# Block rounding laid out by position in the block, with its powers of two held in 16 bits

## The chip, the cores and the metric

The kernel runs on 1 core of one Trainium2 chip. The metric is the device time of one execution in microseconds. The engines are named as in the profile: PE (matrix product; PEld is its weight load), DVE (vector), ACT (scalar), POOL, and SP, which issues DMAs.

## The reference

Two decoder layers run on x, 8 sequences of 256 rows of 512 numbers; each layer has attention, a second mixing and a feed-forward part, each behind a layer norm, each added to x. What is touched here is layer 0's feed-forward part. Its three products round both operands in blocks of 32 numbers along the summed axis: a power of two is taken from the block's largest magnitude, and each element is rounded to a tiny float format at that scale.

```
def _quantize_mx(x, ebits, mfrac, emax_elem, max_norm):
    xb = x.reshape(shp[:-1] + (shp[-1] // BLOCK, BLOCK))          # BLOCK = 32
    amax = jnp.max(jnp.abs(xb), axis=-1, keepdims=True)
    sexp = jnp.floor(jnp.log2(jnp.where(amax == 0, 1.0, amax))) - emax_elem
    scale = jnp.exp2(jnp.clip(sexp, -127.0, 127.0))
    return (_quantize_elem(xb / scale, ebits, mfrac, max_norm) * scale).reshape(shp)

_q_act = lambda x: _quantize_mx(x, 2, 3.0, 2.0, 7.5)
_q_w   = lambda w: _quantize_mx(w, 2, 1.0, 2.0, 6.0)
_mx_linear = lambda x, w: einsum('bsh,oh->bso', _q_act(x), _q_w(w))

gate, up = _mx_linear(x, w_gate), _mx_linear(x, w_up)     # 512 -> 2048
return _mx_linear(silu(gate) * up, w_down)                # 2048 -> 512
```

A permutation of the summed axis leaves the product as it is, so long as both operands have the same one.

## The kernel before

One program interleaves all parts. For each engine a string of letters (`TURNS0`) says which stream of work issues its next step; `side_by_side` follows it. A stream is a generator, and a step is what stands between two `yield`s. So the order of each engine's instructions is fixed when the kernel is built, and semaphores hold an engine where its operand isn't there yet. On DVE, letter g steps the weights' rounding (`Quantised.dve`), f the feed-forward part (`Hidden.dve`), b, d and e the attention, the mixing and the norm beside them. Layer 0 reaches to about 1000 us, layer 1 from about 920 us to the end.

**Weights, once.** `Quantised` takes 12 units of [128, 2048] f32: four of `gate`, four of `up`, four of `down`. SP loads a unit into one of two raw buffers. DVE then works in steps: the maximum of each block (L794), its bounds and the exponent e and inverse (L797 to L801, three small instructions in one step), times the inverse (L805), the element's own exponent (L808, L811), an added and subtracted constant that rounds (L814, L817), and last the lower bound and the block's power of two into `w16`, bf16 (L822). PE transposes `w16` in 16 pieces of 128 columns (L834), ACT copies them out of PSUM (L851). Before it writes `w16`, L822 waits for `w_ps`, PE's transposes of the unit before.

**Activations, 8 sequences.** For each sequence `Hidden.dve` rounds five times 1024 numbers per partition: once the normed rows (two row tiles of 512), and four times half a tile of the product of silu and up. That is 40 roundings. One has two steps. `dve_quantise`: maximum of 32 blocks (L1133), its bounds (L1135), e (L1137), inverse (L1139), and the source times the inverse into `z8`, whose fp8 type does the rounding (L1142). `dve_rounded`: bounds from fp8 to bf16 (L1148), then times e (L1150), which lets PE begin the transposes (L1164, L1192) and then the products (L1178, L1204). e and the inverse are f32, one number for each block, and are read with step 0 along the 32 elements:

```
own(nc.vector.tensor_scalar(dst, self.z8[:, :], 7.5 / 64, -7.5 / 64, ALU.min, ALU.max))
own.wait()
nc.vector.tensor_tensor(blocks(dst), blocks(dst), broadcast(self.e[:, :], 2, BLOCK), ALU.mult
                        ).then_inc(self.s["q_ready"], 1)
```

`own` counts DVE's own instructions, and `own.wait()` holds the next one until they are through. POOL multiplies silu and up (L1296) and hides what attention may not see (L737).

Of the kernel before, what the change touches and what calls it, by code (L numbers as in the profile page):

```python
# [6 lines left out]
BF16 = mybir.dt.bfloat16  # L7
F16 = mybir.dt.float16
FP8 = mybir.dt.float8e4
I32 = mybir.dt.int32  # L10
ALU = mybir.AluOpType
# [138 lines left out]
def build(nc, x, ctx_rows, ctx_cols, A, F, M, G, Xd, out):  # L150
# [17 lines left out]
    with top:  # L168
        def sb(stack, name, shape, dt=F32):
            return stack.enter_context(nc.sbuf_tensor(name, shape, dt))  # L170
# [589 lines left out]
        class Quantised:  # L760


            def __init__(self, st, banks, room, gate16, up16, down16):
                self.b = banks
                self.gate16, self.up16, self.down16 = gate16, up16, down16
                self.raw = [room[:, 2048 * i:2048 * i + 2048] for i in range(2)]
                self.c = room[:, 4096:6144]
                self.w16 = room[:, 6144:7168].bitcast(BF16)
                self.q_max, self.q_e, self.q_inv, _ = (
                    sb(st, f"w_{part}", [P, 2048 // BLOCK])[:, :] for part in ("max", "e", "inv", "sc"))  # L770
                self.raw_in = [sem(f"w_raw_in{i}") for i in range(2)]
# [16 lines left out]
            def dve(self, dve, own, i):  # L788
# [10 lines left out]
                own(nc.vector.tensor_scalar(q_e.bitcast(I32), q_max.bitcast(I32), EXPONENT, None, ALU.bitwise_and))  # L799
                own.wait()  # L800
                mark = own(nc.vector.tensor_scalar(q_inv.bitcast(I32), q_e.bitcast(I32), -1.0, float(256 << 23),  # L801
# [307 lines left out]
        class Hidden:  # L1109


            def __init__(self, st, banks, mixing, room, quantised, gate16, up16, down16):
# [3 lines left out]
                                    for a in range(2))  # L1116
# [7 lines left out]
                self.m, self.e, self.inv, _ = (sb(st, f"ffn_{part}", [P, 1024 // BLOCK])  # L1124
                                                     for part in ("m", "e", "inv", "sc"))
# [4 lines left out]
            def dve_quantise(self, dve, own, src):  # L1130
                m, e, inv = (t_[:, :] for t_ in (self.m, self.e, self.inv))
                blocks = lambda t_: t_.rearrange("p (n b) -> p n b", b=BLOCK)
                own(nc.vector.tensor_reduce(m, blocks(src), AX.X, ALU.max, apply_absolute_value=True))  # L1133
# [3 lines left out]
                own(nc.vector.tensor_scalar(e.bitcast(I32), m.bitcast(I32), EXPONENT, None, ALU.bitwise_and))  # L1137
                own.wait()
                own(nc.vector.tensor_scalar(inv.bitcast(I32), e.bitcast(I32), -1.0, float(250 << 23),  # L1139
                                            ALU.mult, ALU.add))  # L1140
                own.wait()
# [3 lines left out]
            def dve_rounded(self, dve, own, at, dst):  # L1145
                blocks = lambda t_: t_.rearrange("p (n b) -> p n b", b=BLOCK)
# [99 lines left out]
            def dve(self, dve, own, n):  # L1246
# [5 lines left out]
                self.dve_quantise(dve, own, self.xn[:, :, :].rearrange("p t d -> p (t d)"))  # L1252
                yield
                self.dve_rounded(dve, own, 5 * n, self.iq[0][:, 0:1024])
                for g in range(TT * FB + 2):
# [17 lines left out]
                    self.dve_quantise(dve, own, self.inter[q % 2])  # L1273
                    yield
                    self.dve_rounded(dve, own, 5 * n + q + 1, self.iq[T][:, 1024 * half:1024 * half + 1024])
# [764 lines left out]
```

## Time and profile before

| | |
|---|---|
| median of 3 runs | 1605.75 us (1604.0 to 1606.85) |
| the profiled execution | 1603.94 us |
| its span, first to last instruction | 1602.2 us |
| busy in the span | PE 85%, DVE 83%, ACT 65%, POOL 27% |
| the chain that ended last | PE 47%, DVE 29%, ACT 10%, issue 7%, POOL 4% |
| DVE from 15.8 to 1000 us | 866.8 us busy of 984.2 |

The profile is of one execution. Busy time says how full an engine is; the chain of waits, followed back from the last instruction, says which work the end waited for. Both are read by stretch, since the change lies between 15 and 976 us alone.

### The profile page before, as it was taken

The numbers are of one execution on the slowest core, as the hardware profiler recorded it, in microseconds if no ns is written. First come the engines' busy times: TensorE is split into PE (matmuls) and PEld (weight loads), VectorE is DVE, ScalarE is ACT, GpSimd is POOL, SyncE is SP. The second block draws the span as 40 slices with busy tenths as digits, with TensorE's granted clock in tenths as the row PEclk, the third lists the DMA queues.
The fourth block names the chain that finished last, engine by engine and source line by source line (L and its number), as shares of the span: only waits on it lengthen the run. The fifth ranks groups of instructions, "written<-read, shape, count | busy, mean of one in ns | idle before, by whom it ended". The sixth has DMA issues, their size and how long they took to land.

```text
span 1602.2 us, 32850 instructions
## 1 busy us (share of the span) xinstructions
PE 1361.3 (85%) x13068; PEld 745.7 (47%) x13068; DVE 1332.5 (83%) x1965; ACT 1037.2 (65%) x1884; POOL 428.2 (27%) x495
## 2 busy tenths in 40 slices
PE   3778878879899999898978767879999998999986
PEld 2454535344445453444443333446555555555643
DVE  6988989979879888887798899888788888978743
ACT  3244365465673865765695769886899788989431
POOL 1432141132240422321331240241222313122310
PEclk9697989799999999999999988889999999999988
DMA  6313122200201111002120003011020211101020
GB/s 223 93 54 93 34 68 68 74 15 1 75 15 41 36 41 42 21 22 54 63 89 28 1 1 132 20 41 44 2 71 13 59 39 33 41 5 44 2 81 27
DMA packets 54201, 76.24 MB, mean 48 GB/s; under 512 B 8480, under 2 KB 23840, under 8 KB 53536
## 3 DMA queue, kind: packets, MB, share of 16 engines
q1 hardware_dynamic: 54048, 74.14, 16.2%
q8 instruction: 104, 1.70, 0.4%
q14 instruction: 49, 0.40, 0.1%
HBM read 38.98 MB, written 9.44 MB: 30 GB/s over the span
## 4 chain that ended last, share of the span: by engine, by line
PE 47%; DVE 29%; ACT 10%; issue 7%; POOL 4%; DMA 1%; SPq 1%; ACTq 0%; DVEq 0%; POOLq 0%
PE bank L200 16%; DVE mix_NM L1079 4%; PE bank L1178 4%; PE bank L534 3%; DVE ssm_HS L1537 2%; PE bank L542 2%; PE bank L522 2%; PE bank L992 2%; PE bank L1204 2%; PE bank L557 2%; DVE ffn_m L1133 2%; PE bank L977 2%; POOL attn_P L737 2%; PE bank L495 1%; DVE ffn_Z L1142 1%
## 5 line engine op out<-in xcount | busy, mean ns | idle before, releaser
L1052 ACT ACTIVATE mix_P<-bank 128x512 f32<-128x512 f32 x256 | 142.3, 604 | 50.6 <-PE bank L977 50.2
L1079 DVE TENSOR_REDUCE mix_NM<-bank 128x2 f32<-128x512 f32 x256 | 162.8, 682 | 11.2 <-PE bank L952 10.4
L737 POOL TENSOR_SCALAR_AFFINE_SELECT cross_P<-cross_P 128x256 f32<-128x256 f32 x128 | 90.5, 717 | 272.9 <-ACT cross_P L642 272.4
L1296 POOL TENSOR_TENSOR ffn_room<-ffn_room 128x512 f32<-128x512 f32 x64 | 89.9, 1406 | 263.9 <-ACT ffn_room L1235 167.0
L1537 DVE TENSOR_TENSOR_SCAN ssm_HS<-ssm_DA,ssm_DD 128x1024 f32<-128x1024 f32 x64 | 150.3, 2348 | 10.1 <-ACT ssm_DD L1488 5.5
L737 POOL TENSOR_SCALAR_AFFINE_SELECT attn_P<-attn_P 128x256 f32<-128x256 f32 x128 | 89.6, 713 | 243.7 <-ACT attn_P L642 243.7
L1485 ACT ACTIVATE ssm_DA<-ssm_Z,A_T 128x255 f32<-128x255 f32 x256 | 110.9, 498 | 3.1 <-DVE ssm_HS L1537 2.7
L642 ACT ACTIVATE attn_P<-bank 128x384 f32<-128x384 f32 x128 | 63.8, 498 | 63.1 <-PE bank L523 62.7
L642 ACT ACTIVATE cross_P<-bank 128x384 f32<-128x384 f32 x128 | 62.6, 489 | 50.9 <-PE bank L523 50.5
L1543 DVE TENSOR_TENSOR ssm_HS<-ssm_HS,ssm_CS 128x1024 f32<-128x1024 f32 x64 | 82.0, 1281 | 0.9
L1460 ACT ACTIVATE ssm_Z<-bank 128x512 f32<-128x512 f32 x128 | 72.2, 599 | 13.4 <-PE bank L1374 12.8
L1178 PE MATMUL bank<-gate,ffn_XQ 128*128 128x512 bf16 x256 | 68.8, 392 | 13.0 <-DVE ffn_room L1260 12.7
L992 PE MATMUL bank<-mix_P,mix_V 128*32 128x256 f32 x1024 | 69.6, 395 | 2.8 <-DVE mix_XN L1095 2.2
L1178 PE MATMUL bank<-up,ffn_XQ 128*128 128x512 bf16 x256 | 68.5, 392 | 0.5 <-ACT ffn_room L1235 0.5
L977 PE MATMUL bank<-mix_Q,mix_K 64*128 64x256 f16 x512 | 53.2, 288 | 18.3 <-ACT mix_P L1052 15.6
L1488 ACT ACTIVATE ssm_DD<-ssm_Z 128x1024 f32<-128x1024 f32 x64 | 67.2, 1050 | 0.0
L952 PE MATMUL bank<-mix_K,mix_Q 64*128 64x256 f16 x512 | 51.6, 281 | 16.6 <-DVE mix_NM L1079 15.1
L1204 PE MATMUL bank<-down,ffn_room 128*128 128x512 bf16 x256 | 64.9, 389 | 0.0
L1231 ACT ACTIVATE ffn_room<-bank 128x512 f32<-128x512 f32 x64 | 38.9, 607 | 34.3 <-PE bank L1178 34.1
L1260 DVE SCALAR_TENSOR_TENSOR ffn_room<-ffn_room,bank 128x512 f32<-128x512 f32 x64 | 43.5, 680 | 19.3 <-ACT ffn_room L1231 19.3
L522 PE MATMUL bank<-attn_stack 128*128 128x256 f16 x128 | 39.1, 305 | 21.9 <-ACT attn_P L642 16.6
L1150 DVE TENSOR_TENSOR ffn_room<-ffn_room,ffn_e 128x1024 bf16<-128x1024 bf16 x40 | 54.3, 1357 | 1.4
(410 smaller groups left out, 4043.3 us busy)
## 6 DMA issues: line engine op xcount, KB each, us to landing
attn_stack<-attn_P SPq DMA_DIRECT2D x96, 128.0 KB, 2.4
cross_stack<-cross_P SPq DMA_DIRECT2D x96, 128.0 KB, 2.4
ffn_room<-f_gate SPq DMA_DIRECT2D x4, 1024.0 KB, 5.3
XR<-x SPq DMA_DIRECT2D x8, 512.0 KB, 6.8
ffn_room<-f_up SPq DMA_DIRECT2D x4, 1024.0 KB, 5.6
ffn_room<-f_down SPq DMA_DIRECT2D x4, 1024.0 KB, 4.9
x_mid<-XR SPq DMA_DIRECT2D x8, 512.0 KB, 3.0
XR<-x_mid SPq DMA_DIRECT2D x8, 512.0 KB, 3.7
```

The source lines that it names most:

```text
L200: last = nc.tensor.matmul(out, a_, b_, start=(start and i == 0), stop=(stop and i == len(terms) - 1))
L642: nc.scalar.activation(self.p[h % 8][:, :], bank[self.b[0]][:, 0:S + P], ACT.Exp, scale=HD1 ** -0.5).then_inc(self.p_ready, 1)
L737: nc.gpsimd.affine_select(out=diagonal, in_=diagonal, compare_op=ALU.is_ge, fill=0.0, base=0, pattern=[[0, 2], [1, P]], channel_multiplier ...
L977: last = nc.tensor.matmul(bank[b4[i]][:, k * S:(k + 1) * S], self.k[rows, v // 2, k * P:(k + 1) * P], self.q[rows, v, :], start=(k == 0), ...
L992: last = nc.tensor.matmul(bank[b][32 * j:32 * j + 32, half * S:(half + 1) * S], self.v[:, k, g, :], self.p[(4 * g + j) % 8][:, k * S:(k + ...
L1052: nc.scalar.activation(self.p[h % 8], bank[b4[h % 2]][:, :], ACT.Exp, scale=HD2 ** -0.5).then_inc(s["p_ready"], 1)
L1079: nc.vector.tensor_reduce(self.nm[:, t, 16 * i + 2 * g:16 * i + 2 * g + 2], bank[b4[u % 3]][:, :].rearrange("p (c k) -> p c k", c=2), AX.X ...
L1178: last = nc.tensor.matmul(bank[b][:, :], self.xq[:, k, T * P:(T + 1) * P], w[:, k, fb * 512:(fb + 1) * 512], start=(k == 0), stop=(k == DC ...
L1204: last = nc.tensor.matmul(bank[b][:, :], self.iqt[:, f, :], self.down16[:, f, :], start=(f == 0), stop=(f == FC - 1))
L1296: nc.gpsimd.tensor_tensor(self.inter[q % 2][:, 512 * (g % 2):512 * (g % 2) + 512], self.sg[g % 2], self.up[g % 2], ALU.mult).then_inc(s["i ...
L1485: nc.scalar.activation(self.da[:, G % 2, k, 1:S], self.z[:, h, 1:S], ACT.Exp, scale=self.A_T[:, h:h + 1])
L1537: nc.vector.tensor_tensor_scan(flat(self.hs), flat(self.da), flat(self.dd), 0.0, ALU.mult, ALU.add).then_inc(s["hs_ready"], 1)
```

## The change

The elements of a group of blocks are stored by their position in the block: first element 0 of every block of the group, then element 1, and so on. A group is 16 blocks (512 numbers) for the normed rows, `gate` and `up`, and 32 blocks (1024 numbers) for the product of silu and up, and `down`. With this the factor of each block runs along the innermost axis with step 1, and the 32 positions repeat the row.

- e and the inverse are bf16. Their bits are made as 16-bit integers from the upper half of each f32 maximum.
- Activations: the product with the inverse reads the f32 source 32 numbers apart and writes `z8` in order. The bounds are as before. The last product has dst, source and e in bf16, all of step 1. For the normed rows (8 of the 40) the bounds on the maximum are left out (`bounded=True`).
- Weights: the added constant has no upper bound of 6 in it any more (`tensor_tensor` in place of `scalar_tensor_tensor`); the subtraction reads both f32 operands 32 numbers apart and writes bf16 straight into `w16`; a new `tensor_scalar` bounds `w16` on both sides; the last product is bf16 by bf16. The wait for `w_ps` stands before the subtraction, since that is now the first to write `w16`.
- PE, ACT, POOL, SP and `TURNS0` are the same.

```diff
@@ Quantised.__init__
-                self.q_max, self.q_e, self.q_inv, _ = (
-                    sb(st, f"w_{part}", [P, 2048 // BLOCK])[:, :] for part in ("max", "e", "inv", "sc"))
+                self.q_max = sb(st, "w_max", [P, 2048 // BLOCK])[:, :]
+                self.q_e, self.q_inv = (sb(st, f"w_{part}", [P, 2048 // BLOCK], BF16)[:, :] for part in ("e", "inv"))
@@ Quantised.dve
-                own(nc.vector.tensor_scalar(q_e.bitcast(I32), q_max.bitcast(I32), EXPONENT, None, ALU.bitwise_and))
+                own(nc.vector.tensor_scalar(q_e.bitcast(I16), q_max.bitcast(I16)[:, 1::2], EXPONENT >> 16, None,
+                                            ALU.bitwise_and))
...
-                mark = own(nc.vector.scalar_tensor_tensor(y, y, 6.0, c, ALU.min, ALU.add))
-                yield
-                own.wait(mark)
-                mark = own(nc.vector.tensor_tensor(y, y, c, ALU.subtract))
-                yield
+                mark = own(nc.vector.tensor_tensor(y, y, c, ALU.add))
+                yield
+                n = (1024 if self.units[i][1] == "down" else D) // BLOCK
+                positions = self.w16.rearrange("p (a b n) -> p a b n", b=BLOCK, n=n)
+                y_, c_ = (t_.rearrange("p (a n b) -> p a b n", n=n, b=BLOCK) for t_ in (y, c))
                 own.wait(mark)
                 if i:
                     dve.wait_ge(self.w_ps, 2 * i)
-                nc.vector.scalar_tensor_tensor(blocks(self.w16), blocks(y), -6.0, broadcast(q_e, 2, BLOCK), ALU.max,
-                                               ALU.mult).then_inc(self.w16_ready, 1)
+                mark = own(nc.vector.tensor_tensor(positions, y_, c_, ALU.subtract))
+                yield
+                own.wait(mark)
+                own(nc.vector.tensor_scalar(self.w16, self.w16, 6.0, -6.0, ALU.min, ALU.max))
+                own.wait()
+                nc.vector.tensor_tensor(positions, positions, broadcast(q_e.rearrange("p (a n) -> p a n", n=n), 2, BLOCK),
+                                        ALU.mult).then_inc(self.w16_ready, 1)
@@ Hidden.dve_quantise
-                own(nc.vector.tensor_scalar(m, m, TINY, HUGE, ALU.max, ALU.min))
+                if not bounded:
+                    own(nc.vector.tensor_scalar(m, m, TINY, HUGE, ALU.max, ALU.min))
+                    own.wait()
+                own(nc.vector.tensor_scalar(e.bitcast(I16), m.bitcast(I16)[:, 1::2], EXPONENT >> 16, None,
+                                            ALU.bitwise_and))
...
-                nc.vector.tensor_tensor(blocks(self.z8[:, :]), blocks(src), broadcast(inv, 2, BLOCK), ALU.mult,
-                                        saturate=False).then_inc(self.s["z_ready"], 1)
+                nc.vector.tensor_tensor(self.by_position(self.z8[:, :], n), src.rearrange(
+                    "p (a n b) -> p a b n", n=n, b=BLOCK), self.each_position(inv, n), ALU.mult, saturate=False
+                    ).then_inc(self.s["z_ready"], 1)
@@ Hidden.dve_rounded
-                nc.vector.tensor_tensor(blocks(dst), blocks(dst), broadcast(self.e[:, :], 2, BLOCK), ALU.mult
-                                        ).then_inc(self.s["q_ready"], 1)
+                nc.vector.tensor_tensor(self.by_position(dst, n), self.by_position(dst, n),
+                                        self.each_position(self.e[:, :], n), ALU.mult).then_inc(self.s["q_ready"], 1)
```

DVE's instructions at weight unit 1, the second unit, with the semaphores that hold them: before,

```order
L814 SCALAR_TENSOR_TENSOR ffn_room<-ffn_room 128x2048 [waits done_dve]
L679 TENSOR_REDUCE attn_NM<-bank 128x4 [waits attn_rest_ready,attn_s_ps] x4
L683 TENSOR_REDUCE attn_NM<-bank 128x2 [waits attn_s_ps] x8
L817 TENSOR_TENSOR ffn_room<-ffn_room 128x2048 [waits done_dve]
L688 SCALAR_TENSOR_TENSOR attn_NQL<-bank,attn_NQH 32x256 [waits attn_nqh_ready]
L822 SCALAR_TENSOR_TENSOR ffn_room<-ffn_room,w_e 128x2048 [waits w_ps,done_dve]
```

and with the change, where all line numbers are those of the changed kernel:

```order
L816 TENSOR_TENSOR ffn_room<-ffn_room 128x2048 [waits done_dve]
L680 TENSOR_REDUCE attn_NM<-bank 128x4 [waits attn_rest_ready,attn_s_ps] x4
L684 TENSOR_REDUCE attn_NM<-bank 128x2 [waits attn_s_ps] x8
L824 TENSOR_TENSOR ffn_room<-ffn_room 128x2048 [waits w_ps,done_dve]
L689 SCALAR_TENSOR_TENSOR attn_NQL<-bank,attn_NQH 32x256 [waits attn_nqh_ready]
L827 TENSOR_SCALAR ffn_room<-ffn_room 128x2048 [waits done_dve]
L829 TENSOR_TENSOR ffn_room<-ffn_room,w_e 128x2048 [waits done_dve]
```

The wait for `w_ps` has moved from the last instruction of the unit to the subtraction, ahead of the small attention instruction (L688 before, L689 after). The last step has two instructions in place of one.

## Rows read from the trace of the kernel before

**Rows 1.** The page, its sections 1 and 4 (busy times; the chain of waits).
```profile
PE 1361.3 (85%) x13068; PEld 745.7 (47%) x13068; DVE 1332.5 (83%) x1965; ACT 1037.2 (65%) x1884; POOL 428.2 (27%) x495
...
PE 47%; DVE 29%; ACT 10%; issue 7%; POOL 4%; DMA 1%; SPq 1%; ACTq 0%; DVEq 0%; POOLq 0%
```

**Rows 2.** Busy time in three stretches: us, then each engine's busy time (xinstructions).
```profile
core 0: us, PE busy (x) PEld busy (x) DVE busy (x) ACT busy (x) POOL busy (x), PEclk, DMA share, GB/s
15.80:53.00 37.20, 24.39 (x147) 16.08 (x147) 36.75 (x27) 15.27 (x26) 16.35 (x11) 0.91 0.40 127
53.00:370.00 317.00, 251.78 (x2634) 141.77 (x2635) 282.80 (x346) 158.56 (x294) 82.54 (x87) 0.85 0.21 60
370.00:1000.00 630.00, 548.23 (x4984) 271.27 (x4982) 547.27 (x844) 419.07 (x756) 179.14 (x193) 0.97 0.14 41
```

**Rows 3.** The chain of waits by line, from 370 to 1000 us.
```profile
by line: PE bank L1178 10.1%; issue 8.8%; DVE mix_NM L1079 7.9%; PE bank L200 7.6%; PE bank L1204 4.2%; DVE ffn_m L1133 3.8%; PE bank L992 3.6%; DVE ffn_Z L1142 3.5%; DVE ffn_room L1150 3.4%; PE bank L952 2.8%; DVE ffn_room L1148 2.7%; ACT 
```

**Rows 4.** The chain of waits by line, from 15.8 to 53, then from 53 to 370 us.
```profile
by line: DVE ffn_room L805 12.1%; DVE ffn_room L811 12.1%; DVE w_max L794 11.8%; DVE ffn_room L808 9.8%; DVE ffn_room L822 6.2%; DVE ffn_room L814 6.0%; DVE ffn_room L817 5.9%; DVE l_wo_l L292 5.9%; DVE l_wq_l L292 5.9%; DVE l_wk_l L292 5.9
...
by line: PE bank L200 9.4%; issue 8.8%; POOL attn_P L737 7.6%; DVE mix_NM L1079 5.3%; ACT attn_P L642 4.4%; PE bank L522 4.3%; PE bank L534 4.2%; PE bank L542 3.5%; PE bank L992 3.5%; PE bank L495 3.2%; PE bank L977 2.7%; PE bank L834 2.4%;
```

**Rows 5.** Groups of DVE instructions: xcount | busy us, mean ns of one | idle before.
```profile
L1150 DVE TENSOR_TENSOR ffn_room<-ffn_room,ffn_e 128x1024 bf16<-128x1024 bf16 x40 | 54.3, 1357 | 1.4
...
L1133 DVE TENSOR_REDUCE ffn_m<-ffn_room 128x32 f32<-128x1024 f32 x40 | 48.4, 1210 | 2.0 <-ACT ffn_room L357 1.6
...
L1135 DVE TENSOR_SCALAR ffn_m<-ffn_m 128x32 f32<-128x32 f32 x40 | 13.7, 343 | 1.4
```

**Rows 6.** Single lines of the activations' rounding: ns min/median/max, first and last start, forms.
```profile
L1142 DVE TENSOR_TENSOR ffn_Z<-ffn_room,ffn_inv x40: 1224/1225/2274, 367.7 to 974.1; 128x1024 fp8e4<-128x1024 f32 x40
...
L1150 DVE TENSOR_TENSOR ffn_room<-ffn_room,ffn_e x40: 1224/1226/3252, 371.4 to 976.1; 128x1024 bf16<-128x1024 bf16 x40
...
L1148 DVE TENSOR_SCALAR ffn_room<-ffn_Z x40: 628/693/2309, 370.7 to 975.3; 128x1024 bf16<-128x1024 fp8e4 x40
...
L1135 DVE TENSOR_SCALAR ffn_m<-ffn_m x40: 181/182/1307, 367.1 to 973.4; 128x32 f32<-128x32 f32 x40
```

**Rows 7.** The same for lines of the weights' rounding.
```profile
L817 DVE TENSOR_TENSOR ffn_room<-ffn_room x12: 2269/2282/2519, 35.7 to 352.7; 128x2048 f32<-128x2048 f32 x12
...
L822 DVE SCALAR_TENSOR_TENSOR ffn_room<-ffn_room,w_e x12: 2270/2293/4485, 38.0 to 358.3; 128x2048 bf16<-128x2048 f32 x12
...
L811 DVE TENSOR_SCALAR ffn_room<-ffn_room x12: 1162/1220/3252, 27.8 to 343.7; 128x2048 f32<-128x2048 f32 x12
```

**Rows 8.** The same for the scan of the second layer, another kind of work.
```profile
L1537 DVE TENSOR_TENSOR_SCAN ssm_HS<-ssm_DA,ssm_DD x64: 2269/2284/3375, 922.8 to 1484.3; 128x1024 f32<-128x1024 f32 x64
```

**Rows 9.** Timeline round weight unit 1: start us, us, engine, line [idle before <-releaser].
```profile
57.47 5.01 DVE L683 TENSOR_REDUCE attn_NM<-bank 128x2 f32<-128x512 f32 x8
...
61.68 1.03 PE L834 MATMUL bank<-ident,ffn_room 128*128 128x128 bf16 x8
62.39 2.28 DVE L817 TENSOR_TENSOR ffn_room<-ffn_room 128x2048 f32<-128x2048 f32 x1
...
62.94 1.06 PE L834 MATMUL bank<-ident,ffn_room 128*128 128x128 bf16 x8
...
64.59 0.41 DVE L688 SCALAR_TENSOR_TENSOR attn_NQL<-bank,attn_NQH 32x256 f16<-32x256 f32 x1
...
67.72 0.37 PE L522 MATMUL bank<-attn_stack 128*128 128x256 f16 x1 [3.72 <-issue]
```

**Rows 10.** DVE alone in time, one rounding of activations and what stands in it.
```profile
482.95 1.21 DVE L1133 TENSOR_REDUCE ffn_m<-ffn_room 128x32 f32<-128x1024 f32 x1
...
484.84 1.23 DVE L1142 TENSOR_TENSOR ffn_Z<-ffn_room,ffn_inv 128x1024 fp8e4<-128x1024 f32 x1
...
486.58 0.68 DVE L1148 TENSOR_SCALAR ffn_room<-ffn_Z 128x1024 bf16<-128x1024 fp8e4 x1
487.30 1.23 DVE L1150 TENSOR_TENSOR ffn_room<-ffn_room,ffn_e 128x1024 bf16<-128x1024 bf16 x1
```

More of the change, by code:

```diff
@@ L10 @@
 I32 = mybir.dt.int32
+I16 = mybir.dt.int16
 ALU = mybir.AluOpType
@@ L1123, in __init__ @@
                 self.z8 = sb(st, "ffn_Z8", [P, 1024], FP8)
-                self.m, self.e, self.inv, _ = (sb(st, f"ffn_{part}", [P, 1024 // BLOCK])
-                                                     for part in ("m", "e", "inv", "sc"))
+                self.m = sb(st, "ffn_m", [P, 1024 // BLOCK])
+                self.e, self.inv = (sb(st, f"ffn_{part}", [P, 1024 // BLOCK], BF16) for part in ("e", "inv"))
                 names = ("th_ready", "z_ready", "q_ready", "xqt_ps", "xqt_ready", "gu_ps", "silu_ready", "up_ready", "in_done",
@@ L1128, in __init__, with dve_quantise @@
                 self.s = {part: sem(f"ffn_{part}") for part in names}
[L1130 to L1133, printed above, removed]
-                own.wait()
-                own(nc.vector.tensor_scalar(m, m, TINY, HUGE, ALU.max, ALU.min))
+            def dve_quantise(self, dve, own, src, groups, bounded=False):
+                m, e, inv = self.m[:, :], self.e[:, :], self.inv[:, :]
+                n = 1024 // BLOCK // groups
+                own(nc.vector.tensor_reduce(m, src.rearrange("p (n b) -> p n b", b=BLOCK), AX.X, ALU.max,
+                                            apply_absolute_value=True))
+                own.wait()
+                if not bounded:
[3 more added lines that the diff above has]
+                                            ALU.bitwise_and))
@@ L1136, in dve_quantise @@
                 own.wait()
-                own(nc.vector.tensor_scalar(e.bitcast(I32), m.bitcast(I32), EXPONENT, None, ALU.bitwise_and))
+                own(nc.vector.tensor_scalar(inv.bitcast(I16), e.bitcast(I16), -1.0, float(250 << 7), ALU.mult, ALU.add))
                 own.wait()
-                own(nc.vector.tensor_scalar(inv.bitcast(I32), e.bitcast(I32), -1.0, float(250 << 23),
-                                            ALU.mult, ALU.add))
-                own.wait()
-                nc.vector.tensor_tensor(blocks(self.z8[:, :]), blocks(src), broadcast(inv, 2, BLOCK), ALU.mult,
-                                        saturate=False).then_inc(self.s["z_ready"], 1)
@@ L1145, in dve_rounded, with by_position @@
-            def dve_rounded(self, dve, own, at, dst):
-                blocks = lambda t_: t_.rearrange("p (n b) -> p n b", b=BLOCK)
+                nc.vector.tensor_tensor(self.by_position(self.z8[:, :], n), src.rearrange(
+                    "p (a n b) -> p a b n", n=n, b=BLOCK), self.each_position(inv, n), ALU.mult, saturate=False
+                    ).then_inc(self.s["z_ready"], 1)
+            def by_position(self, rows, n):
+                return rows.rearrange("p (a b n) -> p a b n", b=BLOCK, n=n)
@@ L1147, in dve_rounded, with each_position @@
+            def each_position(self, scale, n):
+                return broadcast(scale.rearrange("p (a n) -> p a n", n=n), 2, BLOCK)
+            def dve_rounded(self, dve, own, at, dst, groups):
+                n = 1024 // BLOCK // groups
                 dve.wait_ge(self.s["z_ready"], at + 1)
@@ L1251, in dve @@
                     dve.wait_ge(s["iqt_ps"], 4 * n - 2)
-                self.dve_quantise(dve, own, self.xn[:, :, :].rearrange("p t d -> p (t d)"))
+                self.dve_quantise(dve, own, self.xn[:, :, :].rearrange("p t d -> p (t d)"), TT, bounded=True)
                 yield
-                self.dve_rounded(dve, own, 5 * n, self.iq[0][:, 0:1024])
+                self.dve_rounded(dve, own, 5 * n, self.iq[0][:, 0:1024], TT)
                 for g in range(TT * FB + 2):
@@ L1272, in dve @@
                     dve.wait_ge(s["q_ready"], 5 * n + q + 1)
-                    self.dve_quantise(dve, own, self.inter[q % 2])
+                    self.dve_quantise(dve, own, self.inter[q % 2], 1)
                     yield
-                    self.dve_rounded(dve, own, 5 * n + q + 1, self.iq[T][:, 1024 * half:1024 * half + 1024])
+                    self.dve_rounded(dve, own, 5 * n + q + 1, self.iq[T][:, 1024 * half:1024 * half + 1024], 1)
                     if q == 3:
```

2 lines of the change are left out of this document (1 added, 1 removed).

## The prediction

> **What bounds the kernel now.** First the page: PE and DVE are both busy for over 80% of the span, and the chain that ended last runs 47% over PE and 29% over DVE [rows 1]. No one engine bounds it. All that the change touches lies between 15 and 976 us, so the page's shares are no use and I read stretches. From 15.8 to 53 us DVE is busy 36.75 of 37.2 us, from there to 370 us 282.8 of 317, from 370 to 1000 us 547.27 of 630 [rows 2]: 99%, 89%, 87%. DVE has little room in layer 0, and PE has as little from 370 us on (548.23).
>
> Next, how much of the touched work the end waited for. From 370 to 1000 us the chain spends 3.8% of 630 us, 23.9 us, in L1133 [rows 3], whose 40 instructions take 48.4 us [rows 5]: half of the roundings of activations are on the chain. L1142 (3.5%) and L1150 (3.4%) say the same. For the weights the first 37 us are almost all DVE in the chain, with L817 and L822 at about 6% each, one of either; from 53 to 370 us neither is among the lines listed, the last of which has 2.4% [rows 4], 7.6 us. L817 and L822 have 11 instructions each there, about 25 us, so under three tenths of each.
>
> Last, the durations. An f32 instruction of 1024 numbers takes 1.225 us, one of 2048 2.282 us, so a further number costs 1.03 ns, which I call one beat, and an instruction some 0.17 us besides [rows 6, 7]. L1150 is bf16 into bf16 but has an f32 factor: 1.226 us, one number per beat. L1148, one source, moves 1024 in 0.693 us: two per beat. The scan takes 2.284 us for 1024: two beats per number [rows 8].
>
> **The activations' last product, L1150.** With all three operands 16 bits wide and in runs of 16 or 32, I take two numbers per beat, L1148's 0.69 us. A gain of 0.53 us, 40 times: 21.3 us less on DVE. The other end is 1.226 us and no gain. Its mean is 1.357, not 1.226 [rows 5], so some instances are held up, and that I leave as it is.
>
> **The bounds left out** for 8 of 40: 0.18 us each by the median [rows 6], 1.5 us; by the mean of 0.343 [rows 5], 2.7 us. The integer steps on e and the inverse are as many as before and of the same small size: nothing.
>
> **The product into z8, L1142.** Same operation, same count, but its f32 source is now read 32 numbers, 128 bytes, apart, at each element. No DVE row in this trace does that in SBUF on a large instruction: all go along rows in runs of 16 or more. Lower end: the hop is free and it stays 1.225 us. Upper end: the rate of the scan, two beats, 2.284 us, and for a worse case three beats, about 3.3 us. I take the scan's 2.28 us, that is 1.06 us more. The choice isn't forced by a row; what speaks for it is that wherever more than one number per beat is reached (L1148, L811) neighbours in memory are read, so a read fetches more than one number, and a hop per element wastes that. 40 times 1.06 is 42.4 us more on DVE.
>
> The Trainium skill speaks to this and against the change: "DVE Microarchitecture Reference", section "Measured stream behaviour on trn2", says that a port keeps its full rate only where successive elements come in runs of at least two adjacent 4-byte words, and gives 1.05 ns per column for such runs, 1.73 for one source hopping at each element, and 2.50 where both sources step by 24 words. An estimate by that page: L1142 would cost 0.7 to 1.5 us more in place of 1.06, the weights' subtraction 1.4 to 3.0 us more, and by the same sum as below the kernel would land between 1616 and 1640 us. No row of this trace shows it.
>
> For the activations then: +42.4 - 21.3 - 1.5 = +19.6 us on DVE. Half of the roundings are on the chain: **+9.8 us**. At 482.95 us a rounding stands in a stretch where DVE has no gap between its instructions [rows 10]: what grows there pushes all behind it, so half is the low side for a lengthening. Before a sequence's rounding is late, L1178's and L1204's products on PE are next to be late.
>
> **The weights.** Per unit: L814 loses its bound and keeps its time. L817 reads two hopping sources: by the same choice two beats for 2048, 4.4 us, +2.1 (ends 0 and three beats, +4.2). L822 from 2.293 to 1.22, since two per beat for 2048 is L1142's time for 1024 now: -1.07 (other end 0). The new instruction on bf16 lies between L811's 1.22 us and L1148's 0.69, which would be four per beat; I take 0.70, since one source at 16 bits should have both gains. Sum +1.75 us, 12 times: +21 us on DVE. Unit 0 is on the chain: +1.75. Unit 1's subtraction stands ahead of L688, and that ahead of SP's DMA and of L522, before which PE stands idle for 3.72 us [rows 9]: +2.1 on the chain. The other ten: three tenths of 17.5, +5.3. Together **+9.1 us**.
>
> **The moved wait.** In every unit but unit 1 (and unit 4, by a little) PE's transposes of the unit before were over long before the subtraction. At unit 1 the subtraction starts at 62.39 us and PE's last eight transposes of unit 0 end at 62.94 + 1.06 = 64.00 [rows 9]. The subtraction now waits: +1.6 us, and behind it on DVE wait L688 and so L522. **+1.6 us**. After a slower unit 0 the same wait simply moves along.
>
> **Sum.** 9.8 + 9.1 + 1.6 = 20.5 us on the profiled execution's 1603.94: 1624.4. The median is 1.8 us higher: 1626 us, 1.3% slower. About 0.2% (3 us) is what a measurement of this kernel can tell from no change.
>
> **Rivals.**
> - *The hop is free.* DVE loses 21.3 + 1.5 on the activations, half of it on the chain, -11.4 us; on the weights -0.37 per unit, unit 0 and three tenths of the rest, -1.6 us; the moved wait stays, +1.6. -11.4 us: about 1594, faster. For it: no row shows a slow hop, and the change is only in addresses. It decides if L1142's successor is at 1.23 us; the point of no gain is at about 1.6 us, where the growth of the two hopping instructions eats the rest. Chance 0.18.
> - *The hop costs about half a beat*, and gain and loss cancel on the activations, while the weights bring a few us: 1606 to 1609. Chance 0.07 to be within 0.2%.
> - *The last product isn't faster*, because its factor is a repeated row of 16 or 32: it stays one per beat, with slow hops. 21.3 us come back on DVE, half on the chain, and 1.07 for each weight unit: +10.6 and +4.6. 1641 us. L1148, with two per beat, speaks against it but has no such factor. Chance 0.1.
> - *Three beats*, or DVE's growth of 40 us drags nearly all roundings onto the chain, since it was at 87 to 89%: with all of +19.6 and +21 counted, 1646; with three beats and seven tenths on the chain, 1672. Chance 0.15.
> - The forecast itself, two beats give or take a third: 0.5.
>
> **Range and chances.** The forecast's own case, L1142 at 0.7 to 1.4 us more and the subtraction at twice that, gives by the same sum +10 to +31 us: 1616 to 1637. The range takes in the free hop at its lower end, and at the upper the growth that is on the chain as a whole: 1594 to 1650. Left out are three beats and a free hop with luck. Faster 0.18, same 0.07, slower 0.75.
>
> **What would show it.** In the changed kernel's profile: the z8 product at 2.28 us (free: 1.23), the last product at 0.69 (no gain: 1.23), the weights' subtraction at 4.4 us, its last product at 1.22, the new instruction at 0.70. DVE's busy time up by about 40 us; from 370 to 1000 us its share above 87%, and more of L1133's line in the chain than 3.8%. At weight unit 1 DVE idle for about 1.6 us before the subtraction, released by PE's transposes. The prediction is wrong if the z8 product stays below 1.6 us, or if DVE grows as told and the span doesn't: then the roundings had more slack than the chain's half says.

## The result: 1.6% slower, and the profile after

The changed kernel took 1634.43 us (median of 4 runs, 1633.79 to 1635.03) against 1605.83 us (1604.0 to 1606.85) in the same comparison: ratio 1.0158, interval 1.0136 to 1.018. The forecast was 1626 us, slower; 1634.4 lies in the range of 1594 to 1650. Its profiled execution took 1633.79 us with a span of 1632.1. One of the four executions of the changed kernel with a second buffer (e9, below) took 1954.07 us at a mean granted clock of 0.641, where the others had 0.93, and its ratio leaves it out.

From the page of the changed kernel, busy times and the chain, to set against [rows 1]:

```profile
PE 1370.2 (84%) x13005; PEld 753.6 (46%) x13068; DVE 1353.4 (83%) x1969; ACT 1037.5 (64%) x1884; POOL 440.6 (27%) x495
...
PE 46%; DVE 31%; ACT 9%; issue 8%; POOL 4%; DMA 1%; SPq 0%; ACTq 0%; DVEq 0%; POOLq 0%
```

DVE is busy for 20.9 us more, PE for 8.9 although its work is the same and 63 of its records are missing here (its mean granted clock was 0.939 before and is 0.925 here). DVE's share of the chain has gone from 29 to 31%, which says little: the stretches and the single lines say more. First the touched lines, in the view of one line each (ns min/median/max, first and last start, forms), to set against [rows 6, 7]:

```profile
L1151 DVE TENSOR_TENSOR ffn_Z<-ffn_room,ffn_inv x40: 1880/1930/2910, 389.1 to 999.6; 128x1024 fp8e4<-128x1024 f32 x40
...
L1164 DVE TENSOR_SCALAR ffn_room<-ffn_Z x40: 629/693/2260, 392.7 to 1001.6; 128x1024 bf16<-128x1024 fp8e4 x40
...
L1166 DVE TENSOR_TENSOR ffn_room<-ffn_room,ffn_e x40: 691/693/2717, 393.4 to 1002.3; 128x1024 bf16<-128x1024 bf16 x40
...
L824 DVE TENSOR_TENSOR ffn_room<-ffn_room x12: 3953/4062/4204, 35.8 to 372.5; 128x2048 bf16<-128x2048 f32 x12
...
L827 DVE TENSOR_SCALAR ffn_room<-ffn_room x12: 657/744/3882, 39.9 to 378.9; 128x2048 bf16<-128x2048 bf16 x12
...
L829 DVE TENSOR_TENSOR ffn_room<-ffn_room,w_e x12: 1224/1226/1381, 43.8 to 379.6; 128x2048 bf16<-128x2048 bf16 x12
```

- L1151 is L1142's successor, with the source read 32 numbers apart: 1.930 us for 1.225.
- L1164 is L1148 and unchanged. L1166 is L1150's successor, all bf16 in step 1: 0.693 us for 1.226.
- L824 is L817's successor, two sources apart: 4.062 us for 2.282. L829, the weights' last product: 1.226 for 2.293.
- L827 is the new instruction on bf16: 0.744 us, but once 3.882; its mean, from the view of groups, is 1.17:

```profile
L827 DVE TENSOR_SCALAR ffn_room<-ffn_room 128x2048 bf16<-128x2048 bf16 x12 | 14.1, 1172 | 0.3
```

By medians one rounding of activations grew by 0.705 - 0.533 = 0.17 us, and one weight unit by 1.78 + 0.74 - 1.07 = 1.45 us. So the change gains on every last product what it was built to gain, and pays more than that where the operands are brought into the new order.

Where the time went is read by marks. The first maximum of activations starts at 365.8 us before and at 387.4 after; the last instruction of the last rounding starts at 976.1 [rows 6] and at 1002.3. Busy times in the two stretches, first before, then after (columns as in [rows 2]):

```profile
0.00:365.80 365.80, 272.86 (x2751) 155.30 (x2752) 317.55 (x370) 175.97 (x319) 101.87 (x123) 0.86 0.26 79
365.80:976.10 610.30, 534.40 (x4903) 266.00 (x4902) 528.30 (x833) 398.91 (x730) 179.14 (x193) 0.97 0.12 35
```

```profile
0.00:387.40 387.40, 279.38 (x2751) 159.01 (x2752) 335.68 (x382) 176.26 (x319) 110.57 (x123) 0.84 0.25 75
387.40:1002.30 614.90, 530.53 (x4841) 266.72 (x4902) 530.67 (x825) 398.95 (x731) 184.31 (x193) 0.97 0.12 34
```

Of 29.9 us of span, 21.6 are lost before the first rounding, in the time of the weights, with 18.1 us more DVE work; 4.6 in the roundings' stretch, with 2.4 us more; and 3.7 behind the last one, where the code is the same. Those last I don't take for an effect of the change. The last addition of layer 1, DVE writing `XR` (first and last start), before, after, and in a kernel with the code of before but for two types (below):

```profile
L1726 DVE TENSOR_TENSOR XR<-XR,bank x16: 660/683/690, 1133.5 to 1597.1; 128x512 f32<-128x512 f32 x16
```

```profile
L1742 DVE TENSOR_TENSOR XR<-XR,bank x16: 660/684/689, 1164.1 to 1626.9; 128x512 f32<-128x512 f32 x16
```

```profile
L1727 DVE TENSOR_TENSOR XR<-XR,bank x16: 660/684/689, 1138.1 to 1601.3; 128x512 f32<-128x512 f32 x16
```

From the last rounding to it: 621.0 us before, 624.6 after, 624.7 (1601.3 - 976.6) in the third, whose ratio to before is 1.0011. All eleven other profiles of this case lie between 623.3 and 625.9 us, so the one profile of before happened to have a short layer 1.

The stretches of [rows 2] in the changed kernel, and the chain of waits by line from 53 to 370 and from 370 to 1010 us, to set against [rows 3, 4]:

```profile
core 0: us, PE busy (x) PEld busy (x) DVE busy (x) ACT busy (x) POOL busy (x), PEclk, DMA share, GB/s
15.80:53.00 37.20, 24.97 (x147) 16.45 (x147) 36.82 (x25) 15.32 (x26) 15.96 (x11) 0.95 0.42 132
53.00:370.00 317.00, 242.33 (x2503) 133.84 (x2504) 281.85 (x336) 144.16 (x274) 88.74 (x86) 0.82 0.20 58
370.00:1000.00 630.00, 540.31 (x4930) 274.36 (x4991) 543.54 (x841) 409.75 (x743) 187.19 (x195) 0.96 0.12 34
```

```profile
by line: POOL attn_P L738 9.7%; PE bank L201 8.6%; issue 8.0%; DVE mix_NM L1086 6.8%; DVE ffn_room L824 4.4%; PE bank L535 4.1%; PE bank L496 3.9%; PE bank L543 3.3%; PE bank L485 2.8%; ACT attn_P L643 2.8%; PE bank L558 2.7%; PE bank L999 
...
by line: issue 11.1%; PE bank L1194 9.7%; DVE mix_NM L1086 8.6%; PE bank L201 7.3%; DVE ffn_Z L1151 5.9%; DVE ffn_m L1140 4.5%; PE bank L1220 3.1%; PE bank L959 2.7%; DVE ffn_room L1164 2.7%; ACT mix_P L1059 2.6%; PE bank L999 2.4%; DVE ffn
```

Cut at fixed times the stretches hide the change: DVE is as busy per stretch as before, since the work has moved later. In the chain one sees it: L824 with 4.4% of 317 us is 14 us, where L817 was under 2.4%; L1151 has 5.9% where L1142 had 3.5%, and L1140, the maximum, 4.5% where L1133 had 3.8% (the stretch here ends 10 us later).

DVE's timeline at weight units 0 and 1, to set against [rows 9]:

```profile
35.77 4.06 DVE L824 TENSOR_TENSOR ffn_room<-ffn_room 128x2048 bf16<-128x2048 f32 x1
39.87 3.88 DVE L827 TENSOR_SCALAR ffn_room<-ffn_room 128x2048 bf16<-128x2048 bf16 x1
...
60.98 5.01 DVE L684 TENSOR_REDUCE attn_NM<-bank 128x2 f32<-128x512 f32 x8
67.62 3.97 DVE L824 TENSOR_TENSOR ffn_room<-ffn_room 128x2048 bf16<-128x2048 f32 x1 [1.62 <-PE bank L841]
71.52 0.40 DVE L689 SCALAR_TENSOR_TENSOR attn_NQL<-bank,attn_NQH 32x256 f16<-32x256 f32 x1
```

At unit 1 DVE stands idle for 1.62 us before the subtraction, released by PE's transposes (L841): the moved wait as it was foretold. At unit 0 the new bf16 instruction takes 3.88 us in place of 0.7. In the changed kernel a POOL memset runs beside it:

```profile
39.69 3.51 POOL L408 MEMSET attn_stack<- 32x4096 f16 x1
```

In the old kernel the same memset (L407, from 39.58 us) ran beside L822 and L794, which took their usual 2.29 and 2.28 us. There two instructions of unit 1 were held up instead:

```profile
47.02 2.38 DVE L808 TENSOR_SCALAR ffn_room<-ffn_room 128x2048 int32<-128x2048 int32 x1
49.44 3.25 DVE L811 TENSOR_SCALAR ffn_room<-ffn_room 128x2048 f32<-128x2048 f32 x1
```

Their successors take 1.23 us each here, so about 3.2 us come back; but the small L798 and L803 take 1.63 and 2.22 us for 0.64 and 0.48, which costs 2.7 (L800 between them gives 0.8 back). At the next attention instruction, which started at 54.94 us before and starts at 58.45 here, DVE is 3.5 us later, 2 us more than the 1.45 of the medians. So such hold-ups fall on whichever instruction stands there. That POOL's work beside them is the cause is not shown; no run takes it away.

### The profile page after: what moved, and what is told of

It reads as the page before. It is cut to its first block, busy times and chain, and to the rows that moved or that the text cites. A ratio compares the mean times of both kernels' runs of the same rounds, so it can differ in the third digit from the quotient of the medians.

```text
span 1632.1 us, 32791 instructions
## 1 busy us (share of the span) xinstructions
PE 1370.2 (84%) x13005; PEld 753.6 (46%) x13068; DVE 1353.4 (83%) x1969; ACT 1037.5 (64%) x1884; POOL 440.6 (27%) x495
## 4 chain that ended last, share of the span: by engine, by line
PE 46%; DVE 31%; ACT 9%; issue 8%; POOL 4%; DMA 1%; SPq 0%; ACTq 0%; DVEq 0%; POOLq 0%
PE bank L201 16%; DVE mix_NM L1086 5%; PE bank L1194 4%; PE bank L535 3%; DVE ffn_Z L1151 2%; PE bank L543 2%; DVE ssm_HS L1553 2%; PE bank L496 2%; POOL attn_P L738 2%; PE bank L558 2%; PE bank L523 2%; DVE ffn_m L1140 2%; PE bank L1418 1%; PE bank L999 1%; PE bank L485 1%
## 5 line engine op out<-in xcount | busy, mean ns | idle before, releaser
L1312 POOL TENSOR_TENSOR ffn_room<-ffn_room 128x512 f32<-128x512 f32 x64 | 94.6, 1480 | 263.4 <-ACT ffn_room L1251 181.1
L738 POOL TENSOR_SCALAR_AFFINE_SELECT attn_P<-attn_P 128x256 f32<-128x256 f32 x128 | 96.0, 764 | 250.4 <-ACT attn_P L643 250.3
L1151 DVE TENSOR_TENSOR ffn_Z<-ffn_room,ffn_inv 128x1024 fp8e4<-128x1024 f32 x40 | 78.4, 1959 | 1.4
L1194 PE MATMUL bank<-gate,ffn_XQ 128*128 128x512 bf16 x227 | 63.6, 397 | 15.8 <-DVE ffn_room L1276 11.9
L1220 PE MATMUL bank<-down,ffn_room 128*128 128x512 bf16 x237 | 61.3, 389 | 1.5 <-issue 0.7
```

What stands on the lines that cost most here:

```text
L738: nc.gpsimd.affine_select(out=diagonal, in_=diagonal, compare_op=ALU.is_ge, fill=0.0, base=0, pattern=[[0, 2], [1, P]], channel_multiplier ...
L1151: nc.vector.tensor_tensor(self.by_position(self.z8[:, :], n), src.rearrange("p (a n b) -> p a b n", n=n, b=BLOCK), self.each_position(inv, ...
L1194: last = nc.tensor.matmul(bank[b][:, :], self.xq[:, k, T * P:(T + 1) * P], w[:, k, fb * 512:(fb + 1) * 512], start=(k == 0), stop=(k == DC ...
L1312: nc.gpsimd.tensor_tensor(self.inter[q % 2][:, 512 * (g % 2):512 * (g % 2) + 512], self.sg[g % 2], self.up[g % 2], ALU.mult).then_inc(s["i ...
```

## Experiments

I use the mark again: the start of the last rounding's last instruction, 976.1 us before. It leaves layer 1 out, which differs from run to run, but it is read from one profile of each kernel. The start of the first rounding is the other mark: 365.8 us before. "Over before" is worked out from the ratio.

**Theory A.** DVE is full before 390 us, and each microsecond it grows there is a microsecond of the kernel; the weights make most of the loss. **Theory B.** The activations' roundings, half on the chain, cost as much as the weights. **Theory C.** The moved wait ties DVE to PE's order and costs far more than its 1.6 us.

### The activations' part alone (e1_acts)

```diff
 the changed kernel, with class Quantised (the weights' rounding) as in the kernel before
```

> The activations' part of the change alone; the weights are rounded as before, in natural order, so the summed axes of the two operands no longer correspond. Theory A (DVE's growth before 390 us is what costs, and the weights make it): z8 product 1.93 us, last product 0.69, DVE busy +6 us, time 1606 to 1613 us. Theory B (the activations' roundings are half on the chain and hopping hurts there as much as in the weights): 1618 us or more.

Measured: 1613.27 us, ratio 1.0025 (1.0007 to 1.0044), 4 us over before. The z8 product and the last product:

```profile
L1145 DVE TENSOR_TENSOR ffn_Z<-ffn_room,ffn_inv x40: 1878/1934/2924, 368.2 to 981.4; 128x1024 fp8e4<-128x1024 f32 x40
...
L1160 DVE TENSOR_TENSOR ffn_room<-ffn_room,ffn_e x40: 691/693/2719, 372.5 to 984.1; 128x1024 bf16<-128x1024 bf16 x40
```

The durations are those of the whole change; the mark is 984.1 us, 8.0 later. DVE's busy time is 4.8 us up, 1337.3 for the 1332.5 of [rows 1]. That is A's size and not B's, which asked for 12 us or more.

### The weights' part alone (e2_weights)

```diff
 the kernel before, with class Quantised as in the changed kernel
```

> The weights' part alone; activations as before, in natural order, so the summed axes no longer correspond. Theory A: the first rounding of activations starts about 21 us later than before, time 1622 to 1632 us. Theory B: 1612 to 1618 us.

Measured: 1631.44 us, ratio 1.0137 (1.0115 to 1.0158), 22 us over before.

```profile
L824 DVE TENSOR_TENSOR ffn_room<-ffn_room x12: 3930/4050/4190, 35.7 to 373.2; 128x2048 bf16<-128x2048 f32 x12
...
L1157 DVE TENSOR_TENSOR ffn_room<-ffn_room,ffn_e x40: 1224/1226/3252, 393.8 to 999.0; 128x1024 bf16<-128x1024 bf16 x40
```

The mark is 999.0, 22.9 later. The weights' part makes the loss; B falls.

### The types without the order (e3_types)

```diff
-                self.m, self.e, self.inv, _ = (sb(st, f"ffn_{part}", [P, 1024 // BLOCK])
-                                                     for part in ("m", "e", "inv", "sc"))
+                self.m = sb(st, "ffn_m", [P, 1024 // BLOCK])
+                self.e, self.inv = (sb(st, f"ffn_{part}", [P, 1024 // BLOCK], BF16) for part in ("e", "inv"))
```

and e and the inverse made from 16-bit integers, as in the change.

> Before, with e and the inverse of the activations in bf16 but in natural order, the factor at step 0 along the 32 elements. If type alone gives two numbers per beat: last product 0.69 us, DVE busy -21 us, 1590 to 1600 us. If step 1 is needed (my theory): last product stays 1.226 us, z8 product 1.225 us, time within 3 us of before.

Measured: 1608.4 us, ratio 1.0011 (0.9994 to 1.0028), no difference.

```profile
L1143 DVE TENSOR_TENSOR ffn_Z<-ffn_room,ffn_inv x40: 1224/1225/2289, 368.4 to 974.6; 128x1024 fp8e4<-128x1024 f32 x40
...
L1151 DVE TENSOR_TENSOR ffn_room<-ffn_room,ffn_e x40: 1224/1226/3248, 372.0 to 976.6; 128x1024 bf16<-128x1024 bf16 x40
```

With the factor in bf16 but repeated at step 0 the last product stays at 1.226 us. The 0.693 needs the factor to run at step 1 (the change and the next run have it so), and the new order provides that.

### The same in pairs (e4_pairs, and once more)

The order is: pair of positions, block, element of the pair. Each f32 read then takes two neighbours before it hops, and e holds each value twice so that it still runs at step 1. Each instruction keeps three free dimensions, so the normed rows take two z8 products of 512, and a weight unit two or four subtractions. The weights have the same order, with PE and ACT as in the change.

```diff
-                own(nc.vector.tensor_scalar(e.bitcast(I16), m.bitcast(I16)[:, 1::2], EXPONENT >> 16, None,
-                                            ALU.bitwise_and))
+                own(nc.vector.tensor_scalar(e.bitcast(I16).rearrange("p (n t) -> p n t", t=2),
+                                            broadcast(m.bitcast(I16)[:, 1::2], 2, 2), EXPONENT >> 16, None,
+                                            ALU.bitwise_and))
...
-                nc.vector.tensor_tensor(self.by_position(self.z8[:, :], n), src.rearrange(
-                    "p (a n b) -> p a b n", n=n, b=BLOCK), self.each_position(inv, n), ALU.mult, saturate=False
-                    ).then_inc(self.s["z_ready"], 1)
+                for a in range(groups):
+                    part = slice(a * 1024 // groups, (a + 1) * 1024 // groups)
+                    last = nc.vector.tensor_tensor(
+                        self.z8[:, part].rearrange("p (b n t) -> p b n t", n=n, t=2),
+                        src[:, part].rearrange("p (n b t) -> p b n t", n=n, t=2),
+                        broadcast(inv[:, 2 * n * a:2 * n * (a + 1)].rearrange("p (n t) -> p n t", t=2), 1, BLOCK // 2),
+                        ALU.mult, saturate=False)
```

> The change with pairs of neighbouring elements kept together: the order is pair of positions, block, element of the pair, and e has each value twice. If the hop at each element is what slows the reads: z8 product 1.23 us for 1024 numbers, two of 0.69 for the normed rows, subtraction in pieces of 0.69 (512) or 1.23 us (1024), last products 0.69 and 1.23 us; DVE busy about 20 us below before and the time 1590 to 1603 us. If any order out of line costs: z8 product stays at 1.9 us and the time at 1630 us or above.

> The kernel with pairs once more, beside the next one: 0.988 to 0.993 of before.

Measured: 1593.54 us, ratio 0.9903 (0.988 to 0.9925); the second time 1596.4 us, 0.9932 (0.9906 to 0.9959). **Faster than before by 0.7 to 1.0%.** The new bf16 instruction, the weights' last product, the z8 product, and the activations' last product:

```profile
L831 DVE TENSOR_SCALAR ffn_room<-ffn_room x12: 672/694/1878, 38.4 to 359.1; 128x2048 bf16<-128x2048 bf16 x12
...
L834 DVE TENSOR_TENSOR ffn_room<-ffn_room,w_e x12: 1224/1226/1303, 40.3 to 359.8; 128x2048 bf16<-128x2048 bf16 x12
...
L1159 DVE TENSOR_TENSOR ffn_Z<-ffn_room,ffn_inv x48: 680/1224/2268, 368.3 to 961.3; 128x1024 fp8e4<-128x1024 f32 x32, 128x512 fp8e4<-128x512 f32 x16
...
L1176 DVE TENSOR_TENSOR ffn_room<-ffn_room,ffn_e x40: 691/693/2716, 372.0 to 963.3; 128x1024 bf16<-128x1024 bf16 x40
```

The z8 product is back at 1.224 us and the last products keep their gain. So it is the hop at every element that costs, not the order as such. Before the first rounding and from there to the last:

```profile
0.00:366.60 366.60, 271.86 (x2752) 154.88 (x2753) 318.22 (x411) 175.62 (x319) 96.55 (x123) 0.86 0.26 79
366.60:963.30 596.70, 529.34 (x4910) 264.78 (x4908) 507.00 (x833) 398.19 (x730) 176.61 (x193) 0.99 0.12 35
```

Up to the first rounding nothing is gained (318.2 us of DVE work for 317.6, since the subtraction in pieces and the new instruction use up what the last product gives). The roundings' stretch has 21.3 us less DVE work than before and is 13.6 us shorter: about two thirds of what DVE is relieved of passes into the time. PE's granted clock is 0.99 there for 0.97 before, so a part of the 13.6 may be PE's.

### The moved wait alone (e5_wait)

```diff
                 own.wait(mark)
+                if i:
+                    dve.wait_ge(self.w_ps, 2 * i)
                 mark = own(nc.vector.tensor_tensor(y, y, c, ALU.subtract))
                 yield
                 own.wait(mark)
-                if i:
-                    dve.wait_ge(self.w_ps, 2 * i)
```

> Before, with the wait for w_ps moved ahead of the weights' subtraction and nothing else. If the wait costs what the timeline shows: DVE idle 1.6 us at unit 1, first rounding of activations 1.5 to 4 us later, time 1 to 4 us over before. If the moved wait is what made most of the 21 us (rival: it ties DVE to PE's order): 10 us or more over before.

Measured: 1611.04 us, ratio 1.0016 (0.9997 to 1.0034). DVE's wait (us in total, times, longest), and the last product:

```profile
DVE ffn_room L819 <- PE bank L834: 2.0, 2, 1.6
...
L1150 DVE TENSOR_TENSOR ffn_room<-ffn_room,ffn_e x40: 1224/1226/3249, 377.2 to 980.9; 128x1024 bf16<-128x1024 bf16 x40
```

The stall is the foretold one. The mark is 980.9, 4.8 later, by one profile; the ratio gives 2.6 us, and its interval reaches from nothing to 5.5. C, with 10 us and more, falls.

The 4.8 us are more than DVE's 2.0 us of waiting, and the timelines show where the rest comes in. A unit's maximum (L794) starts at 83.88 us before and at 85.81 here, 1.9 later; its product with the inverse (L805) at 97.13 and at 103.36, 6.2 later. The delay stays at about 6 up to the first rounding (371.6 for 365.8). From 80 to 100 us PE runs at its lower clock level for all 20 us (granted 0.50), where before it had 0.83; in the 20 us ahead of that it was busy for 12.2 us here and for 12.8 before. Before, then with the moved wait:

```profile
80.00:100.00 20.00, 14.12 (x214) 8.63 (x214) 12.93 (x13) 8.89 (x16) 7.34 (x10) 0.83 0.35 107
```

```profile
80.00:100.00 20.00, 14.43 (x180) 8.47 (x184) 9.73 (x9) 6.47 (x14) 8.58 (x11) 0.50 0.32 106
```

The same 64 small matmuls of attention take 1.95 us before and 3.64 here, and DVE's longest wait for PE (L692) grows from 6.0 to 8.6 us:

```profile
93.13 1.95 PE L557 MATMUL bank<-attn_RC,ident 128*32 128x128 f32 x64 [1.08 <-DVE attn_RC L692]
```

```profile
97.67 3.64 PE L557 MATMUL bank<-attn_RC,ident 128*32 128x128 f32 x64 [1.08 <-DVE attn_RC L692]
```

So a shift of DVE by 2 us went with a longer stretch at the lower clock, and that cost more than the shift. Whether it comes so in every execution isn't measured.

### The growth alone (e6_growth), and both (e7_growth_wait)

```diff
-                mark = own(nc.vector.tensor_tensor(y, y, c, ALU.subtract))
+                own(nc.vector.tensor_tensor(y, y, c, ALU.subtract))
+                own.wait()
+                mark = own(nc.vector.tensor_tensor(c[:, 0:1300], y[:, 0:1300], c[:, 0:1300], ALU.add))
```

> Before, with one more contiguous f32 instruction of 1300 numbers (about 1.5 us) behind the subtraction of each of the 12 weight units, result unused. No hop, no moved wait. If DVE is full there and its growth passes on whole: 12 times 1.5 = 18 us later first rounding, time 16 to 20 us over before. If three tenths are on the chain, as the prediction had it: 5 to 8 us over.

Measured: 1625.15 us, ratio 1.0101 (1.0075 to 1.0128), 16 us over before. The added instruction, and the last product:

```profile
L819 DVE TENSOR_TENSOR ffn_room<-ffn_room x12: 1511/1512/3705, 38.0 to 367.1; 128x1300 f32<-128x1300 f32 x12
...
L1152 DVE TENSOR_TENSOR ffn_room<-ffn_room,ffn_e x40: 1224/1226/3249, 384.9 to 994.6; 128x1024 bf16<-128x1024 bf16 x40
```

12 times 1.5 us are 18 us of plain contiguous work. The first rounding starts at 379.4, 13.6 us later and not the 18 that were expected; the mark is at 994.6, 18.5 later; the time is 16 us over, by its interval 12 to 21. **Most or all of the growth passes into the time**, though the old kernel's chain had less than three tenths of this work on it. The 4.9 us between the two marks arise where the code is the same and DVE's work too (528.0 us for 528.3). PE is busy for 5.9 us more there with as many matmuls, at a granted clock of 0.96 for 0.97:

```profile
379.40:994.60 615.20, 540.26 (x4903) 268.00 (x4901) 528.01 (x833) 398.78 (x730) 180.43 (x193) 0.96 0.12 34
```

> Both of the last two. If growth and wait are all that the weights' part is: within 3 us of the run with the weights' part alone, that is 19 to 24 us over before. If it stays 5 us or more below that run, the hop has a further effect besides its length.

Measured: 1630.77 us, ratio 1.0145 (1.0112 to 1.0179), against 1.0137 for the weights' part.

```profile
L1152 DVE TENSOR_TENSOR ffn_room<-ffn_room,ffn_e x40: 1224/1226/3249, 387.9 to 997.8; 128x1024 bf16<-128x1024 bf16 x40
```

The mark is 997.8, 1.2 us short of the weights' part alone. In the time, growth in length and the wait are enough to account for the weights' part. The first rounding, though, starts at 382.4 us here and at 388.2 there. From it to the mark this kernel takes 615.4 us and that one 610.8, with the same DVE work (527.9 and 527.0 us); PE is busy for 539.9 and 535.5 us, at a granted clock of 0.96 and 0.97, so the clock goes with the second difference. What makes the first, with 0.84 in both, stays open, and with it whether the hop has a small further effect there.

### A second buffer, so that the wait is gone (e9_after_two_buffers, e8_pairs_two_buffers)

```diff
-                self.w16 = room[:, 6144:7168].bitcast(BF16)
+                w16 = room[:, 6144:7168].bitcast(BF16)
+                other = down16[:, 0:4, :].rearrange("p f k -> p (f k)")
+                self.w16s = [other if i < 8 and i % 2 else w16 for i in range(12)]
...
-                    dve.wait_ge(self.w_ps, 2 * i)
+                    dve.wait_ge(self.w_ps, 2 * i - (2 if i < 8 else 0))
```

> The changed kernel, with a second w16 for units 1, 3, 5 and 7 (in the part of down16 that isn't filled yet), so that the moved wait asks for the unit before the last. If the moved wait costs on the chain: DVE no longer idle before the subtraction at unit 1, first rounding of activations 2 to 5 us earlier, 1629 to 1633 us. If the wait was covered anyway: within 1 us of the changed kernel.

Measured: ratio 1.0143 (1.0108 to 1.0178, from three executions), against 1.0158 (1.0136 to 1.018) for the change as it was.

```profile
L1168 DVE TENSOR_TENSOR ffn_room<-ffn_room,ffn_e x40: 691/692/2716, 391.3 to 1003.1; 128x1024 bf16<-128x1024 bf16 x40
```

DVE no longer waits for PE at the subtraction, and the first rounding starts at 385.3 us, 2.1 earlier; but the mark is 1003.1, 0.8 later.

> Pairs and the second w16 together. If the moved wait is what pairs had left over in the weights: first rounding of activations 2 to 4 us earlier than with pairs alone, and 0.986 to 0.990 of before, the fastest of all. If not: the same as with pairs alone.

Measured: 1592.32 us, ratio 0.9913 (0.9883 to 0.9942), beside 0.9932 (0.9906 to 0.9959) for pairs alone, measured next to it. The expected 0.986 to 0.990 isn't reached, and the first rounding starts at 365.8 us, only 0.8 to 1.0 earlier than with pairs alone and not 2 to 4.

```profile
L1178 DVE TENSOR_TENSOR ffn_room<-ffn_room,ffn_e x40: 691/692/2716, 371.3 to 961.8; 128x1024 bf16<-128x1024 bf16 x40
```

The mark is 961.8, against 963.3 and 964.5 for pairs alone. A gain of 2 us would look like this, and so would chance. What the wait costs stays open between nothing and 5 us.

## Why the prediction was right, and where its sizes were off

- **What bounds the kernel.** Right in what it read: DVE with no room in layer 0. It then didn't use it, see the weights.
- **The last product, L1150**, 0.69 us, 21.3 us less on DVE: right, 0.693. Types alone don't give it (e3), the step does. The rival that it stays at one per beat fell.
- **The bounds left out**: 8 instructions of 0.18 us; too small to show by themselves.
- **The z8 product, L1142.** Expected 2.28 us by the scan, between 1.225 and 3.3: it is 1.930. The direction and the place were right, the term was mis-sized: +0.705 in place of +1.06, 28 us in place of 42. The choice of the scan's rate had only the argument that a read fetches more than one number; e4 bears that argument out. The free hop, 1594 us, is refuted.
- **By the Trainium skill**, "Vector Engine (DVE) Microarchitecture Reference", section "Measured stream behaviour on trn2", one source hopping 4 KiB at each element costs 1.73 ns a column; here, with hops of 128 bytes, (1.930 - 0.17) / 1024 us is 1.72 ns, in agreement. For two sources it has 1.76 with long hops and 2.50 with steps of 24 words; with steps of 32 words these runs show (4.062 - 0.17) / 2048, 1.90 ns. Its rule that runs of two neighbours go at the full rate agrees with e4's 1.224 us.
- **The activations' sum**, +9.8 us from +19.6 of DVE work: DVE work grew by 4.8 us, and alone they cost 4 us (1 to 7). The size of the hop made the sum too large. Whether a half is the right share isn't settled: 4 of 4.8 us fits a half and the whole alike, and by the mark, 8.0 us later, it would be more than the whole.
- **The weights' sum**, +9.1 us: the failing step. The subtraction was to grow by 2.1 us a unit and grew by 1.78; the new instruction was right at the median (0.744) and, since it is held up at times, not at the mean (1.17); the last product was right, 1.226. The DVE work of +21 us was near the 18.1 measured. But "the other ten: three tenths" was wrong: of e6's 18 us of growth 13.6 have passed through by the first rounding and 18.5 by the mark, 16 (12 to 21) in the time; three tenths would have been 5 to 8. My reading is that what was off the chain in one execution mostly had less slack than the 1.5 us by which each unit grew; no run measures the slack itself. The rows on how full DVE is stood in the prediction, 282.8 of 317 us busy, and they should have outweighed the chain's share, which priced this lengthening far too low. PE's clock, for which the prediction had no term, moved with it (e5, e6); what it alone is worth isn't measured.
- **The moved wait**: foretold at 1.6 us with its place, measured as 1.62 us of idle time at that place. What it costs in time isn't settled; the 4.8 us of e5's one profile are more than the stall, with PE at the lower clock behind it.
- **The rivals.** The free hop and the last product without gain are refuted. The hop at half a beat, with gain and loss cancelling on the activations, is nearly what the activations do (+0.17 us each), though the hop is two thirds of a beat. Growth that goes onto the chain as a whole, there priced for both parts at 1646 us (with the moved wait it would be 1648), comes nearest for the weights alone. Two of the rivals' times don't come out of the prediction's own terms: a hop of half a beat gives about 1610 us in place of 1606 to 1609, and three beats with seven tenths of the activations on the chain about 1669 in place of 1672. The forecast doesn't use them.
- **The sum.** 9.8 + 9.1 + 1.6 = 20.5 us against 28.6. The parts alone measure 4 and 22, 26 together; two errors of opposite sign, about 6 us too much for the activations and 11 too little for the weights and their wait. That the forecast came within 9 us is partly luck: with the activations' sum right and the weights' as it was, it would have been some 14 off.
- **The signs.** DVE's busy time rose by 20.9 us and not by about 40, and its share from 370 to 1000 us is 86.3%, not above 87%. The maximum's line in the chain (4.5%) and the idle time at unit 1 came as told. Neither of the two signs of being wrong came in: the z8 product isn't below 1.6 us, and the span grew by more than DVE's work.

## What to carry to other kernels

A layout that makes a product's operands dense moves the cost to whichever instruction changes the order, so price that one first, and keep at least two neighbouring 4-byte words together in it: in pairs the same idea turned +1.6% into -0.7 to -1.0%. When an instruction gets longer on an engine that is busy for nine tenths of a stretch, count most or all of its growth there, whether the chain of waits names it or not (here 13.6 of 18 us by the stage's end, 16 in the time). A delay can also shift the stretches in which PE has its lower clock, so compare the granted clock by stretch before a few microseconds are put down to the delay itself. When a new first writer appears for a buffer, the wait for its readers moves ahead of it; read from the timeline which instances it will catch.

## What the runs showed of the hardware that was not expected

- The hop costs 0.69 ns a number with one f32 source 128 bytes apart and 0.87 ns with two: less than the second beat that I had taken, and two hopping sources are only a little dearer than one.
- A bf16 product whose factor is repeated at step 0 along the row takes 1.226 us for 1024 numbers, the same as with an f32 factor; one whose factor is a row of 16, 32 or 64 read again and again takes 0.693.
- Bounds on 2048 bf16 numbers, one source, take 0.657 us at best and 0.694 at the median with pairs: four numbers a beat. But a single instance took 3.88 us in the changed kernel, beside a POOL memset.
- A DVE wait of 2.0 us in all (e5) was followed by 20 us with PE at a granted clock of 0.50 in place of 0.83, in which DVE fell back by another 4.3 us.
